# An eight-stage transformer kernel on one core: batch steps of the 64-wide attention at new places, and a shorter front of the attention with decay

## The reference

```
x += attention_rms(LN(x))        # 16 heads of 8, query and key rms-normed
x += experts_top2(LN(x))
x += attention_decay(LN(x))      # 16 heads of 8, see below
x += experts_top2(LN(x))
x += attention_relative(LN(x))   # bias by bucket of distance
x += experts_choice(LN(x))
x += attention_wide(LN(x))       # 16 heads of 64, see below
x += experts_choice(LN(x))
```

```
q = l2norm(x Wq) * q_scale ; k = l2norm(x Wk) * k_scale ; v = x Wv
attn = softmax(q k / 8) ; x += (attn v) Wo + bo
```

## Time and profile before

| | us |
|---|---|
| median of 3 runs | 5602.24 |
| lowest, highest | 5595.87, 5605.10 |
| the profiled execution's own time | 5598.34 |
| its span | 5596.5 |
| busy: PE, DVE, ACT, POOL | 4584.3, 3680.8, 3464.9, 1407.4 |

### The profile page before, as it was taken

One profiled execution on the slowest core, in us unless ns is written; L12 is line 12 of the kernel. 1 busy time (PEld: TensorE's weight loads), 2 busy tenths in 40 slices (PEclk: granted clock), 3 DMA queues, 4 the chain that ended last, 5 costly groups with the idle time before them and its releaser, 6 DMA issues. The chain is left out here.

```text
span 5596.5 us, 97013 instructions
## 1 busy us (share of the span) xinstructions
PE 4584.3 (82%) x31060; PEld 2303.6 (41%) x31060; DVE 3680.8 (66%) x7243; ACT 3464.9 (62%) x5541; POOL 1407.4 (25%) x1422
## 2 busy tenths in 40 slices
PE   6999859568989976968888758699989989989758
PEld 2222359524444436932222245233333333333345
DVE  5443464477777776457777771777877777777671
ACT  5999745425555545547888723566767766766523
POOL 1101047524334305732233047000000000000037
PEclk8999979779999987979999878799999999999978
DMA  3222222213233322232223233100000000000133
GB/s 86 66 52 67 59 52 50 72 57 90 87 94 88 94 60 61 49 97 57 58 54 66 58 66 55 51 1 0 0 0 0 0 0 0 0 0 0 41 63 55
DMA packets 228307, 266.50 MB, mean 48 GB/s; under 512 B 36906, under 2 KB 194442, under 8 KB 221640
## 3 DMA queue, kind: packets, MB, share of 16 engines
q1 hardware_dynamic: 184468, 195.51, 13.1%
q0 software_dynamic: 43520, 66.97, 6.7%
HBM read 164.90 MB, written 96.65 MB: 47 GB/s over the span
## 5 line engine op out<-in xcount | busy, mean ns | idle before, releaser
L4037 ACT ACTIVATE prob_wide<-slot_wide,peak_wide 128x1024 f32<-128x1024 f32 x512 | 544.4, 1120 | 72.2 <-PE slot_wide L3898 70.8
L2184 ACT ACTIVATE prob_decay<-slot_decay 128x640 f32<-128x640 f32 x512 | 358.7, 705 | 342.2 <-PE slot_decay L2031 341.0
L1000 ACT ACTIVATE prob_rms<-slot_rms 128x1024 f32<-128x1024 f32 x512 | 504.1, 1092 | 56.2 <-PE slot_rms L834 53.8
L2518 DVE TENSOR_TENSOR slot_decay<-slot_decay,dtab_decay 128x512 f32<-128x512 f32 (+3 forms) x1024 | 454.0, 493 | 128.4 <-PE slot_decay L2010 108.4
L1000 ACT ACTIVATE prob_relative<-slot_relative 128x1024 f32<-128x1024 f32 x512 | 497.8, 1049 | 40.9 <-PE slot_relative L834 39.4
L1373 DVE TENSOR_TENSOR prob_relative<-prob_relative,rtab_relative 128x1024 f32<-128x1024 f32 (+1 forms) x256 | 394.9, 1548 | 134.8 <-ACT prob_relative L1000 126.6
L3913 PE MATMUL obank_wide<-prob_wide,v_wide 128*64 128x512 f32 x2048 | 467.7, 598 | 2.4 <-DVE zT_wide L4198 2.4
L3898 PE MATMUL slot_wide<-qT_wide,kT_wide 64*128 64x512 f16 x3072 | 401.3, 390 | 16.0 <-ACT prob_wide L4037 13.5
L4222 POOL TENSOR_TENSOR X<-X,bo_t_wide 128x512 f32 (+1 forms) x16 | 20.3, 1268 | 1562.6 <-DVE xn_wide L198 1542.3
L4184 DVE TENSOR_TENSOR sums_wide<-sums_wide,prob_wide 128x1024 f32<-128x1024 f32 x256 | 312.5, 1221 | 14.6 <-ACT prob_wide L4037 1.3
L858 PE MATMUL obank_relative<-prob_relative,vaug_relative 128*32 128x512 f32 x2048 | 275.8, 611 | 40.1 <-DVE prob_relative L1373 38.6
(11 more groups left out here) (893 smaller groups left out, 10382.6 us busy)
## 6 DMA issues: line engine op xcount, KB each, us to landing
scratch_decay<-parts_decay SPq DMA_DIRECT2D x192, 128.0 KB, 2.4
qst_decay<-scratch_decay SPq DMA_DIRECT2D x128, 128.0 KB
scratch_rms<-parts_rms SPq DMA_DIRECT2D x96, 128.0 KB
kst_rms<-scratch_rms POOLq DMA_DIRECT2D x96, 128.0 KB, 5.5
kst_decay<-scratch_decay SPq DMA_DIRECT2D x192, 64.0 KB
kin_decay<-scratch_decay SPq DMA_DIRECT2D x192, 64.0 KB
scratch_relative<-parts_relative SPq DMA_DIRECT2D x96, 128.0 KB
kst_relative<-scratch_relative POOLq DMA_DIRECT2D x96, 128.0 KB, 6.3
```

The source lines that it names most:

```text
L1000: nc.scalar.activation(prob[:, Q % 2, p:G:2, at:at + m], slot[:, u % 3].rearrange("p (k c) -> p k c", k=2)[:, :, 0:m], ACT.Exp).then_inc(e ...
L2184: nc.scalar.activation(prob[:, Q % 2, j, 0:c1 - c0], slot[:, u % 3, c0:c1], ACT.Exp).then_inc(exp_done, 1)
L2518: last = nc.vector.tensor_tensor(sl, sl, dtab[:, h, 0:m], ALU.mult)
L4037: nc.scalar.activation(prob[:, Q % 2, u % 4, :], slot[:, u % 2, :], ACT.Exp, scale=peak[:, 1:2]).then_inc(exp_done, 1)
```

## The change

In the decay stage: the statistics of tiles 0 to 3 and the first pass (BN_STATS) of tiles 4 to 27 stand ahead of DVE's wait for the loads, the first pass of tiles 28 to 63 behind `TURN_X`, the second pass (`SPREADS`) ahead of `ROOT` 0 and the roots (`ROOTS`) behind `EXT`. ACT computes table rows 0 to 5 behind the QKV steps and 6 to 15 behind `LNEXP`; ACT multiplies by `bias_scale` at `TABLES`, and one DVE operation behind the guard masks the own block (`MASK`). The guard's matmuls take only the keys in use, PE adds the mask by two matmuls of 128 columns, and three transfers bring the maxima straight into the query operand. One constant is no longer loaded.

In the wide stage: largest absolute values by one operation, `scale_values` and `scale_scores` behind `TURN_X` of the front, and other places for the batch steps, with a new place M between the third and the fourth `S` of a block; `Z` stands ahead of M.

```diff
 first_part (decay):
+            if decay: yield "SUMS_OF", EARLY, T        # EARLY = 7 * TPB, behind TURN_X
+                yield "TABLE", 0, 6                     # behind QKV
+                yield "SPREADS",                        # behind MID 1
                 yield "ROOT", 0
                 yield "LNEXP",
+                yield "TABLE", 6, H
                 yield "ROOT", 1
                 yield "EXT",
+                yield "ROOTS",
-            yield "STATS", 1
             yield "TABLES",
 schedule (decay):
             yield "START",
             yield "GUARD",
+            if not prev:
+                yield "MASK",
 SP, guard:
-   sp.dma_start(shifts.rearrange("j r t -> r j t"), gturn[:]).then_inc(guard_stored, 16)
-   sp.wait_ge(guard_stored, 16)
-   sp.dma_start(qst[KR:KS], shifts.rearrange("j (h b) t -> j h (b t)", h=H)).then_inc(guard_moved, 16)
+   for j in range(3):
+       sp.dma_start(qst[KR + j:KR + j + 1].rearrange("a h (b t) -> a (h b) t", t=P),
+                    gturn[:, j, :]).then_inc(guard_moved, 16)
 PE, guard:
+   keys = (qb + 1) * P
    for k in range(2):
-       ... kst[0:KR, 2 * m + k, :], start=True, stop=True
+       ... kst[0:KR, 2 * m + k, 0:keys], start=True, stop=False
+   for k in range(2):
+       last = nc.tensor.matmul(slot[:, i % 3, k * S + keys - P:k * S + keys], negb[:], identb[:],
+                               start=False, stop=True)
 DVE, guard:
-   chain(nc.vector.tensor_tensor(own, own, nega[:]..., ALU.add))
    nc.vector.reduce_max(...)
 ACT, TABLES:
+   for h in range(H):
+       nc.scalar.activation(dtab[:, h, :], dtab[:, h, :], ACT.Copy, scale=bs_t[:, h:h + 1])
 DVE, MASK:
+   own = dtab[:, :, 0:P]
+   link(nc.vector.tensor_tensor(own, own, past[:, 0:P]..., ALU.mult)); dve.sem_inc(ready, 1)

 wide stage:
-HALVES_AT = {(1,"A"):(0,0), (1,"B"):(0,1), (1,"C"):(1,0), (2,"A"):(1,1), (2,"C"):(2,0), (3,"A"):(2,1), (3,"B"):(3,0), (3,"C"):(3,1)}
-NORMS_AT = {(1,"C"):0, (2,"B"):1, (3,"B"):2, (4,"A"):3}
-TURNS_AT = {(4,"B"):0, (4,"C"):1, (5,"A"):2, (5,"C"):3, (6,"A"):4, (6,"C"):5, (7,"A"):6, (7,"C"):7}
-VALUES_AT = {(0,"B"):(0,1), (0,"C"):(2,3)}
+HALVES_AT = {(1,"A"):(0,0), (1,"C"):(0,1), (2,"A"):(1,0), (2,"C"):(1,1), (3,"A"):(2,0), (3,"C"):(2,1), (4,"A"):(3,0), (4,"C"):(3,1)}
+NORMS_AT = {(2,"A"):0, (3,"A"):1, (4,"A"):2, (5,"A"):3}
+TURNS_AT = {(5,"B"):0, (5,"C"):1, (6,"A"):2, (6,"M"):3, (6,"C"):4, (7,"A"):5, (7,"M"):6, (7,"C"):7}
+VALUES_AT = {(0,"B"):(0,), (0,"M"):(1,), (0,"C"):(2,3)}
-            if Q == 6 and place == "B":
+            if Q == 5 and place == "A":
                 yield "Y", 0
                 yield "S", 4 * Q + 2
-                yield "S", 4 * Q + 3
                 if pv:
                     yield "Z", (Q - 1) % C
+                yield from bench_steps(Q, "M", prev, nxt)
+                yield "S", 4 * Q + 3
 DVE, front:
-   reduce_max, tensor_reduce(min), scalar_tensor_tensor
+   reduce_max(..., apply_absolute_value=True)            # Wq, Wk, Wv and the head scales
-   WEIGHTS: scale_values(); low_weights(4); low_weights(5); scale_scores()
+   WEIGHTS: low_weights(4); low_weights(5)
+   TURN_X (batch -1), at its end: scale_values(); scale_scores()
```

More of the change, by code:

```diff
@@ L1900, in do @@
                     o = b - 1
-                    if step == "START" and at_start(b, 0):
+                    if step == "MASK":
                         pe.wait_ge(ready, READY)
@@ L2109, in _ @@
                     nc.scalar.copy(lw[:], obank[:, 0:256]).then_inc(setup_act, 1)
-                    act.wait_ge(setup_dve, 3)
-                    for h in range(H):
-                        nc.scalar.activation(dtab[:, h, :], ahead, ACT.Exp, scale=lnd[:, 0, h:h + 1]
-                                             ).then_inc(tab_act, 1)
                 def do(b, step, *a):
@@ L2174, in do @@
                             act.wait_ge(tab_act, H)
+                        act.wait_ge(tab_act, 2 + H)
+                        for h in range(H):
+                            nc.scalar.activation(dtab[:, h, :], dtab[:, h, :], ACT.Copy, scale=bs_t[:, h:h + 1]
+                                                 ).then_inc(tab_act, 1)
                         act.sem_inc(ready, 1)
+                    if step == "TABLE":
+                        act.wait_ge(setup_dve, 3)
+                        for h in range(*a):
+                            nc.scalar.activation(dtab[:, h, :], ahead, ACT.Exp, scale=lnd[:, 0, h:h + 1]
+                                                 ).then_inc(tab_act, 1)
                     if step == "S":
@@ L2298, in _, with sums_of, spreads_of, roots_of @@
                     dve.sem_inc(setup_dve, 1)
+                def sums_of(tiles):
+                    for t in tiles:
+                        last = nc.vector.bn_stats(stats[:, t, 0:6], X[:, t, :])
+                    link(last)
+                def spreads_of(tiles):
+                    for t in tiles:
+                        last = nc.vector.bn_aggr(stats[:, t, 6:8], stats[:, t, 0:6])
+                    link(last)
+                def roots_of(st):
+                    link(nc.vector.tensor_scalar(st[:, :, 8], st[:, :, 7], 1e-5, None, ALU.add))
+                    rsqrt(nc, link, st[:, :, 9], st[:, :, 8], st[:, :, 10])
+                    dve.sem_inc(stats_ready, 1)
+                statistics(nc, link, X[:, 0:TPB], stats[:, 0:TPB], TPB)
+                dve.sem_inc(stats_ready, 1)
+                sums_of(range(TPB, EARLY))
                 dve.wait_ge(loaded, LOADED)
@@ L2317, in _ @@
                                             ALU.subtract).then_inc(setup_dve, 1)
[L2319 to L2325 removed]
+                link(nc.vector.tensor_copy(negb[:], negf))
+                link(nc.vector.tensor_copy(identb[:], ident[:]))
                 if relative:
@@ L2334, in do @@
                         link.restart()
-                    if step == "STATS":
-                        if rms:
-                            dve.wait_ge(x_second if a[0] else x_first, 16)
-                        at = slice(a[0] * TPB, T if decay and a[0] else (a[0] + 1) * TPB)
-                        statistics(nc, link, X[:, at], stats[:, at], at.stop - at.start)
-                        dve.sem_inc(stats_ready, 1)
-                        if decay and a[0] == 0:
-                            link(nc.vector.tensor_copy(negb[:], negf))
-                            link(nc.vector.tensor_copy(identb[:], ident[:]))
-                            decay_table(range(H // 2))
-                    if step == "EXT" and at_start(b, -1):
-                        decay_table(range(H // 2, H))
-                    if step == "SUMS":
-                        if rms and a[0] == 1:
-                            dve.wait_ge(x_rest, 16 * (NB - 2))
-                        tiles = range(2 * TPB * a[0], 2 * TPB * (a[0] + 1))
-                        for t in tiles:
-                            last = nc.vector.bn_stats(stats[:, t, 0:6], X[:, t, :])
-                        link(last)
-                        for t in tiles:
-                            last = nc.vector.bn_aggr(stats[:, t, 6:8], stats[:, t, 0:6])
-                        link(last)
-                    if step == "ROOTS":
-                        st = stats[:, 2 * TPB:T]
-                        link(nc.vector.tensor_scalar(st[:, :, 8], st[:, :, 7], 1e-5, None, ALU.add))
-                        rsqrt(nc, link, st[:, :, 9], st[:, :, 8], st[:, :, 10])
-                        dve.sem_inc(stats_ready, 1)
+                    if step == "SUMS_OF":
+                        sums_of(range(*a))
+                    if step == "SPREADS":
+                        spreads_of(range(TPB, T))
+                    if step == "ROOTS":
+                        roots_of(stats[:, TPB:T])
+                    if step == "MASK":
+                        dve.wait_ge(tab_act, 2 + 2 * H)
+                        own = dtab[:, :, 0:P]
+                        link(nc.vector.tensor_tensor(own, own, past[:, 0:P].unsqueeze(1).to_broadcast([P, H, P]),
+                                                     ALU.mult))
+                        dve.sem_inc(ready, 1)
                     if step == "NRM" and rms:
@@ L2509, in do @@
                                                   ).then_inc(setup_dve, 1)
-                        dve.sem_inc(ready, 1)
+                            dve.sem_inc(ready, 1)
                     if step == "I":
```

57 lines of the change are left out of this document (21 added, 36 removed).

## The result

The changed kernel takes 5558.52 us (median of 4 runs, 5555.07 to 5560.45) beside 5599.06 for the kernel before on the same chip: ratio 0.9928, 95% interval 0.9914 to 0.9942, so 32 to 48 us less. Forecast were 5490 and a range of 5446 to 5540. The direction is right; a little over a third of the gain came. The profiled execution took 5560.45 us.

A forecast was written before the change was run, and what follows sets the result against it. PE was taken as the busiest engine, so its waits were sought. From 5598.3 us, wide batches took 62, the wide front 11.7 and the decay front 35.7: 5489, taken as 5490; range 5446 to 5540.

The forecast's parts named there:

- Wide batches, first part: Wide batch from the end of Y 1 to TURN 0: DVE sets the pace, 40.0 us becomes 46.6.
- Second part: Wide batch from TURN 0 to the next Y 1's end: PE sets the pace, 66.3 us becomes 55.6.
- Rival 1: Wide batches: the new wait ahead of Y 0 lowers the clock each batch, 1.7 us each, 5514 in all; chance 0.22.
- Wide front: Wide stage's start up to TURN 0: one-operation maxima and moved scales save 11.7 us, bounds 6 and 13.
- Decay front: Decay stage's start to its first scores: earlier guard start and faster guard save 35.7 us, bounds 27 and 40.
- (a): Decay front: ACT's copy of the turned x comes 8.7 us earlier, with early statistics under the loads' landing.
- (c): Decay front: EXT, no longer beside the table's multiplications, takes 5.0 us beside ROOTS, 1.7 less; 6.7 by the contention rule.
- (e): Decay front: the guard's 32 iterations take 25.6 us at PE's pace instead of 38.5, 12.9 less; bounds 24 and 31.
- rival 5: Decay guard: not faster, as small matmuls at the low clock pace it; 13 us of gain gone, 5503; chance 0.08.
- (f): Decay front, from the guard's maxima to the first scores: 9.3 us, no change taken, bounds -2 and +2.

The follow-up runs named there:

- e4: The changed kernel with Z behind the bench steps of place M, instead of ahead of them: 5522.19 us, ratio 0.9862.
- e7: The changed kernel with the edits of e4 and e6, and score unit 21 of each wide batch run three times: 5511.70 us, ratio 0.9842.
- e3: The changed kernel with score units 27 and 31 of every wide batch run three times, useless work filling two waits: 5523.17 us, ratio 0.9867.
- e16: e7 with the guard of the kernel before in the looped decay batches, the new one in batches 0 and 13 to 15: 5503.59 us, ratio 0.9822.
- e13: e7 without the guard's body in the looped decay batches, where it never runs with these inputs: 5493.40 us, ratio 0.9807.
- e15: The kernel before with 128 more waits on a semaphore already there in PE's guard body: 5598.32 us, ratio 0.9997.
- e1: The kernel before with only the wide batch's new places, including M and Y 0's: 5588.59 us beside 5597.64, ratio 0.9982.
- e6: The changed kernel with early decay statistics reordered: 28 first passes, then second passes and root of the first four tiles: 5550.86 us, ratio 0.9909.
- e11: The changed kernel with score units 27 and 31 of every wide batch run twice, not three times as in e3: 5530.00 us, ratio 0.9876.
- e8: The kernel before with score units 16 and 17 of each wide batch run three times: 5595.95 us, ratio 0.9996.

## Why the prediction was wrong, step by step

**Wide batches, first part (46.6 us forecast).** 47.5, 0.9 more. The new wait of 1 to 3 us ahead of Y 0 is there, 2.69; TURN 0's is under 1. Right in mechanism.

**Second part (55.6).** 58.3 in after. In e4 and e7 the same stretch takes 55.4, with the clock at its full level. So the sum of work and the two waits of 1.7 us were right, and the batch without falls is 102.9 against 102.2 forecast. **The step that failed** is the one sentence under it: that the 1.7 us of the low clock go with the 6.1 us wait. The falls didn't go; two of 3.4 us came, behind the waits that I had computed myself. They cost 2.9 us a batch, 44 us over 15 batches. Together with 0.7 us of the rest a batch, 10 us, that makes up the 53 us between -62 and -8.9. A reading was wrong as well: the prediction took 0.66 over 10 us for 3.4 us at the lower level, and it is 6.8. Its price of 1.7 us came near the truth by luck, because almost half of that fall lies in the wait and costs nothing.

**Rival 1** had the mechanism, a wait of each batch that brings the clock down again, and I gave it 0.22. It had the place wrong (ahead of Y 0; in after there is no fall at all there, while in e3 and e4 that same wait brings one in three and in six of fourteen batches) and the number: one fall a batch where there are two. Its price for one, 1.7 us, is right: a batch of e3 with one fall takes 1.6 us more than the others. Its argument against, "Y 0 and PV 4 follow without a gap", looked at what follows a wait. The rule of the Trainium skill (TensorE: Matmul & The Clock Gate, HAM oscillation), that a wait repeated in each round can put PE at half rate every round, is told there of longer waits for transfers. The trace after agrees for waits of 1.79 and 1.89 us, in every one of its batches; e7, where 1.38 us repeats in every batch, shows no fall.

**Wide front (-11.7).** -12.1. The maximum by absolute value took 1.22 us in one operation, as priced. (The terms given for what remains behind NORM 2 add up to 7.6 us, not to 7.4.)

**Decay front (-35.7).** -30.8. (a) The copy of the turned x comes 5.2 us earlier, not 8.7: the early statistics, counted as covered, were held by POOL's memsets. (c) EXT took 3.4 us beside `ROOTS`, less than the 5.0 that I took and far from the 6.7 that I had drawn from the page's rule; but POOL's next instruction held a step of `ROOTS` for 1.94 us and the ones behind it, so the rest of the parts came late, and the guard began 17.9 us sooner instead of 22.8. The prediction asked what contention does to POOL, never what it does to DVE. The Trainium skill (GPSIMD Engine Reference, 1. Specifications) says that GpSimd contends with DVE instructions that have two SBUF inputs or run in a two-port performance mode. The trace agrees for the steps of `ROOTS` with two inputs (1.94 us for 0.30); whether the held TENSOR_SCALARs run in such a mode, no run here shows. (e) The guard's maxima took 27.8, forecast 25.6, under the 31 that I had called decisive: 3.42 us a cycle of four, PE's 3.2 and a wait of 0.2 for DVE. So the guard's maxima took 10.7 us less where 12.9 were forecast, and rival 5 is out. (f) 7.6, forecast 9.3.

**The decay batches (+14.5)** weren't in the sum at all. I took code that no edit touches for code that costs the same; the edit made the guard's body longer in every looped batch, and there are four gaps instead of one, with falls behind them. With the old body back in the loop this stretch takes 846.6 us (e16) instead of 855.0 (e7), beside 842.6 before: the body is shown for 8 of these 12 us, the other 4, with the gap in batch 14, are not explained. Two more falls stand in batches without a gap (the two from 1586 on take 54.6 us).

**Open.** Without the guard's body in the loop (e13), and with the body of before (e16), only the gap at the loop's jump back is left inside the loop; with more waits in the new body there are up to 13 gaps in all, yet before bears 128 more waits with one (e15). So the new body is shown to be needed for the looped gaps, and the pairs show that a place in the program decides which batches have them; how length and place work together isn't shown, nor is theory G's reason, that the jump lands on instructions that aren't fetched. Nor is it settled why the wait ahead of Y 0 brings the clock down in some batches of e3 and e4 and in none of after. Its length doesn't decide alone: it is 2.7 us in all of them. In after, and in e1 and e6, batches and falls alike repeat every 105.8 us; in e3, with batches of 102.8, the fall at Y 0 comes in every fourth. So the moment of a wait seems to count beside its length.

## What to carry to other kernels

When a schedule is made fuller, list the waits that are left by their length, and ask of each whether the clock falls behind it: here the falls behind two of 1.8 us cost 2.9 us a batch, and filling them with work that nobody needs made the kernel 35 us faster. Price what an edit does to code that is skipped: putting the old conditional body back in a loop gave 8 us, though neither body is ever run there. And where work is moved under another engine's, look from both sides at who holds whom.

## What the runs showed of the hardware

- The granted clock fell for 3.4 us behind waits of 1.79 and 1.89 us in an otherwise busy PE (after, in every batch), and in no batch behind 1.15 and 1.23 us (e11), pairs of 1.14 and 0.86 (e7) or a single 1.38 (e7). Behind one and the same wait of 2.69 us it fell in none of after's batches, in three of e3's fourteen, and in six of fourteen in e4 and in e11.
- A fall costs what work it covers: in the kernel before 6.8 us with 3.6 under work, in e8 mostly 3.4 all under work, and no difference in time (ratio 0.9996). One fall of 3.4 us under work cost 1.6 us (e3).
- A TENSOR_SCALAR of 4 or 16 elements a lane on DVE took up to 3.53 us instead of 0.17: it ended within 0.04 us of the end of POOL's running instruction, in the four cases read (after, e6). bn_stats and bn_aggr beside the same memsets weren't held.
- A conditional body that is skipped in a loop, with the load of its flag, cost 0.5 us a batch with no mark in the profile (e13), and gaps of about 3 us in some batches, at the same places of the code in both passes, which the profile ends with "issue". The loop's jump back has such a gap in every trace, 2.8 us with no body in the loop (e13) and 5.8 in the kernel before.
